# A stand-alone normalisation, from features on partitions to tokens on partitions, in a four-layer kernel

## What is computed

```python
def _layernorm(x, axis=-1, eps=1e-05):
    m = jnp.mean(x, axis=axis, keepdims=True)
    v = jnp.var(x, axis=axis, keepdims=True)
    return (x - m) / jnp.sqrt(v + eps)
...
    h = _layernorm(x, axis=-1) * (1 + cb) + sb
    x = x + gb * _L3_ffn_ref(h, L3_ffn_w_router, L3_ffn_w1, L3_ffn_w2, L3_ffn_w3)
```

## Time and profile before

| | us |
|---|---|
| median of 3 executions | 3686.21 |
| lowest, highest | 3654.16, 3691.45 |
| profiled execution, its own time | 3667.89 |
| its span in the trace | 3666.1 |

### The profile page before, as it was taken

The page is one execution under the profiler, slowest core; times in us unless marked ns, Lnnn a source line. Parts: engine busy times, 40 slices in busy tenths (PEclk is TensorE's granted clock), DMA queues, the critical chain, the costliest instruction groups (busy, mean ns, idle before and its releaser), DMA issues. The chain is left out here.

```text
span 3666.1 us, 70823 instructions
## 1 busy us (share of the span) xinstructions
PE 2720.9 (74%) x20756; PEld 1809.7 (49%) x20756; DVE 2283.8 (62%) x5534; ACT 1324.2 (36%) x3004; POOL 1106.0 (30%) x1121
## 2 busy tenths in 40 slices
PE   5888534228788887878488886888799944478899
PEld 3665433216566565367355554666344711155344
DVE  5776761148888785422367766775555689955455
ACT  1566201005555553323156642564322211123221
POOL 2332107733434332546422223332000244411000
PEclk9999765558999998889679996999899955589999
DMA  3332303334333320346311103331000000000000
GB/s 71 52 49 35 118 36 61 43 78 61 48 47 48 46 38 30 141 104 114 78 24 25 24 11 40 46 51 38 2 1 0 1 3 0 0 7 24 4 0 23
DMA packets 154677, 148.84 MB, mean 41 GB/s; under 512 B 29433, under 2 KB 135555, under 8 KB 149379
## 3 DMA queue, kind: packets, MB, share of 16 engines
q1 hardware_dynamic: 118882, 121.52, 17.1%
q0 software_dynamic: 34336, 21.83, 4.2%
q10 hardware_dynamic: 1152, 1.61, 0.1%
HBM read 52.70 MB, written 33.01 MB: 23 GB/s over the span
## 5 line engine op out<-in xcount | busy, mean ns | idle before, releaser
L569 ACT ACTIVATE a1PR<-bank 128x384 f32<-128x384 f32 x512 | 242.4, 492 | 149.0 <-PE bank L626 145.8
L792 DVE TENSOR_REDUCE a1NM<-bank 128x3 f32<-128x384 f32 x512 | 263.0, 548 | 28.7 <-PE bank L608 27.0
L795 DVE TENSOR_REDUCE a2NMQ<-bank 128x2 f32<-128x512 f32 x256 | 168.3, 685 | 65.5 <-PE bank L612 65.3
L959 PE MATMUL bank<-ONES 128*128 128x256 bf16 x960 | 167.9, 281 | 23.4 <-DMA f3nWR<-in_wr 3.9
L569 ACT ACTIVATE a2PR<-bank 128x512 f32<-128x512 f32 x256 | 149.7, 596 | 96.4 <-PE bank L630 94.3
L1515 POOL TENSOR_TENSOR lM<-lF,lV 128x1024 f32<-128x1024 f32 x32 | 122.2, 3818 | 166.8 <-DVE lF L1528 166.3
L792 DVE TENSOR_REDUCE a4NM<-bank 128x3 f32<-128x384 f32 x256 | 136.1, 552 | 54.8 <-PE bank L608 53.3
L792 DVE TENSOR_REDUCE a0NM<-bank 128x3 f32<-128x384 f32 x256 | 136.8, 553 | 49.4 <-PE bank L608 46.4
L624 PE MATMUL bank<-a1QH,a1KH 128*128 128x128 bf16 x512 | 116.0, 228 | 57.0 <-ACT a1PR L569 42.2
L569 ACT ACTIVATE a4PR<-bank 128x384 f32<-128x384 f32 x256 | 121.2, 489 | 93.9 <-PE bank L626 93.0
L2163 POOL DMA_INDIRECT routed<-yY,yID x80 | 123.6, 1545 | 86.5 <-DMA routed<-yY,yID 40.0
(11 more groups left out here) (676 smaller groups left out, 8708.7 us busy)
## 6 DMA issues: line engine op xcount, KB each, us to landing
yWT<-in_w SPq DMA_DIRECT2D x40, 256.0 KB, 3.0
a1QH<-a1SPL SPq DMA_DIRECT2D x96, 64.0 KB
a1KH<-a1SPL SPq DMA_DIRECT2D x96, 64.0 KB
a1QH<-a1QH SPq DMA_DIRECT2D x96, 64.0 KB
a1KH<-a1KH SPq DMA_DIRECT2D x96, 64.0 KB
rows_by_slot<-gZB SPq DMA_DIRECT2D x5, 1040.0 KB
yXG<-rows_by_slot SPq DMA_DIRECT2D x40, 130.0 KB, 3.1
sums<-rZT SPq DMA_DIRECT2D x2, 2112.0 KB
```

Of the source, the lines that this page charges most:

```text
L569: nc.scalar.activation(PR[:, h % 8, :], bank[2 + h % 2][:, 0:NC], ACT.Exp, scale=SCALE)\
L792: v.tensor_reduce(NM3[:, h, :], S_BANK[h % 3][:, 0:NC].rearrange("p (n k) -> p n k", n=3), AX, ALU.max, negate=True).then_inc(s_used.sem, 1)
L795: v.tensor_reduce(NMQ[:, :, h], S_BANK[h % 3][:, 0:NC].rearrange("p (n k) -> p n k", n=2), AX, ALU.max, negate=True).then_inc(s_used.sem, 1)
L959: pe.matmul(bank[7][:, 0:2 * P], spare[:, 0:P], spare[:, :], start=True, stop=True)
```

## The change

`norm_phase` works with tokens on partitions. A group is 512 tokens (four squares of 128x128), NG = 8 groups. For group g TensorE turns the four squares in (transposition from SRC to PSUM: two squares to EVEN_BANK, three banks deep, two to ODD_BANK, two deep). VectorE takes batch-norm statistics of each square (`bn_stats`: six numbers a token, then `bn_aggr`: mean and variance) and adds eps (VE); without mean it uses variance plus squared mean, in two instructions. POOL raises four columns to -0.5 (RS). VectorE makes NR = -mean x RS, then normalises squares 0 and 1 straight from PSUM as (x - mean) x RS; ScalarE does squares 2 and 3 as x x RS + NR. TensorE turns the four results back (OUT_BANK, two deep), and ScalarE writes the result from PSUM with scale and shift, in two instructions of 256 tokens. Logits, where there are any, are computed from the result, four squares at a time (eight passes), and copied by VectorE. The matmuls of `busy` are gone, everything is unrolled, and only ScalarE (before its first scaling) and TensorE (before its first logits) wait for the phase's loads. Nothing outside `norm_phase` is changed.

```diff
@@ -914,28 +914,26 @@
     nc, bank, SRC, centered = c.nc, c.bank, cfg["nsrc"], cfg["ncentered"]
     E = cfg.get("E", 0) if LG is not None else 0
+    F, NG = 2 * T, NB // 2
+    EVEN_BANK, ODD_BANK, OUT_BANK, LG_BANK = bank[0:3], bank[3:5], bank[5:7], bank[7]
+    place = lambda g, n: (EVEN_BANK[g % 3] if n < 2 else ODD_BANK[g % 2])[:, n % 2 * P:(n % 2 + 1) * P]
     with ExitStack() as ctx:
         sb = lambda name, shape, dt=F32: c.sb(cfg["name"] + "n" + name, shape, dt, ctx)
-        XC, SQ, XN = sb("XC", [P, 4, T]), sb("SQ", [P, 2, T]), sb("XN", [P, T])
-        H = sb("H", [P, 4, T])
...
+        ST, MV = sb("ST", [P, 4, 6]), sb("MV", [P, 2, 4, 2])
+        MM, VE, RS, NR, XN = sb("MM", [P, 4]), sb("VE", [P, 2, 4]), sb("RS", [P, 2, 4]), sb("NR", [P, 2, 4]), sb("XN", [P, 2, 4, P])
         COL, WR = sb("COL", [P, 2]), sb("WR", [P, max(E, 1)])
-        S = signals(c, n_mean=int(centered), n_xc=int(centered), n_sq=1, n_var=1, n_ve=1, n_rs=1, n_dg=1, n_bc=1, n_xn=1,
-                    n_h=1, n_copied=1, n_logits=int(E > 0), n_lg=int(E > 0))
...
+        S = signals(c, n_in=2, n_st=4, n_mv=4, n_ve=1 if centered else 2, n_rs=1, n_nr=1, n_xv=1, n_xa=1, n_out=1, n_h=2,
+                    n_logits=int(E > 0), n_lg=int(E > 0))
+        turned_in, st, mv, ve, rs, nr, xv, xa, turned_out, hr, logits, lg = S
         w_in = c.sem(cfg["name"] + "n_w_in")
         loads = ([(COL[:, 0:1], cfg["ngain"])] if cfg.get("ngain") else []) \
             + ([(COL[:, 1:2], cfg["nshift"])] if cfg.get("nshift") else []) + ([(WR[:, :], cfg["wr"])] if E else [])
-        has = lambda stage, t: not isinstance(t, int) or 0 <= t + stage < NB
-
...
+
+        def gains(b):
+            if cfg.get("ngain"):
+                return COL[:, 0:1], (COL[:, 1:2] if cfg.get("nshift") else 0.0)
+            l, k = cfg["layer"], cfg["nmod"]
+            return c.MOD[:, l, k + 1, one(b)], c.MOD[:, l, k, one(b)]
         block = ctx.enter_context(nc.Block())
@@ -948,116 +946,104 @@
         @block.tensor
         def _(pe):
-            if loads:
-                pe.wait_ge(w_in, 16 * len(loads))
...
+            for t in range(NG + 4):
+                g = t
+                if g < NG:
+                    after(pe, xv, g - 3)
+                    for n in range(4):
+                        if n == 2:
+                            after(pe, xa, g - 2)
+                        mm = pe.transpose(place(g, n), SRC[:, g * F + n * P:g * F + (n + 1) * P], c.ID)
+                        if n % 2:
+                            mm.then_inc(turned_in.sem, 1)
+                g = t - 2
+                if 0 <= g < NG:
+                    after(pe, xv, g)
+                    after(pe, hr, g - 2)
+                    for n in range(4):
+                        if n == 2:
+                            after(pe, xa, g)
+                        mm = pe.transpose(OUT_BANK[g % 2][:, n * P:(n + 1) * P], XN[:, g % 2, n, :], c.ID)
+                    mm.then_inc(turned_out.sem, 1)
+                g = t - 4
+                if E and 0 <= g:
+                    if g == 0:
+                        pe.wait_ge(w_in, 16 * len(loads))
+                    after(pe, hr, g)
+                    after(pe, lg, g - 1)
+                    for n in range(4):
+                        mm = pe.matmul(LG_BANK[:, n * E:(n + 1) * E], NT[:, g * F + n * P:g * F + (n + 1) * P], WR[:, :],
                                        start=True, stop=True)
                     mm.then_inc(logits.sem, 1)
-            steps(pe, step)
         @block.gpsimd
         def _(pool):
-            def step(t, m):
-                if has(-1, t):
...
+            for g in range(NG):
+                after(pool, ve, g)
+                after(pool, xv, g - 2)
+                after(pool, nr, g - 2)
+                nc.gpsimd.tensor_tensor(RS[:, g % 2, :], VE[:, g % 2, :], c.HALF[:, 0:4], ALU.pow).then_inc(rs.sem, 1)
         @block.scalar
         def _(act):
-            def step(t, m):
-                if has(0, t):
...
+            for t in range(1, NG + 3):
+                g = t - 1
+                if g < NG:
+                    after(act, nr, g)
+                    after(act, turned_out, g - 2)
+                    for n in (2, 3):
+                        made = nc.scalar.activation(XN[:, g % 2, n, :], place(g, n), ACT.Identity,
+                                                    bias=NR[:, g % 2, n:n + 1] if centered else 0.0, scale=RS[:, g % 2, n:n + 1])
+                    made.then_inc(xa.sem, 1)
+                g = t - 3
+                if 0 <= g:
+                    if g == 0 and loads:
+                        act.wait_ge(w_in, 16 * len(loads))
+                    after(act, turned_out, g)
+                    for n in range(2):
+                        scale, shift = gains(2 * g + n)
+                        nc.scalar.activation(NT[:, tok(2 * g + n)], OUT_BANK[g % 2][:, n * T:(n + 1) * T], ACT.Identity, bias=shift, scale=scale)\
+                            .then_inc(hr.sem, 1)
         @block.vector
         def _(v):
-            if loads:
-                v.wait_ge(w_in, 16 * len(loads))
...
+            for t in range(NG + 4):
+                g = t
+                if g < NG:
+                    after(v, mv, g - 1)
+                    for n in range(4):
+                        if n % 2 == 0:
+                            after(v, turned_in, g, n // 2 + 1)
+                        v.bn_stats(ST[:, n, :], place(g, n)).then_inc(st.sem, 1)
+                    after(v, xv, g - 2)
+                    for n in range(4):
+                        after(v, st, g, n + 1)
+                        v.bn_aggr(MV[:, g % 2, n, :], ST[:, n, :]).then_inc(mv.sem, 1)
+                g = t - 1
+                if 0 <= g < NG:
+                    after(v, rs, g)
+                    after(v, xa, g - 2)
+                    v.scalar_tensor_tensor(NR[:, g % 2, :], MV[:, g % 2, :, 0], -1.0, RS[:, g % 2, :], ALU.mult, ALU.mult).then_inc(nr.sem, 1)
+                    after(v, turned_out, g - 2)
+                    for n in (0, 1):
+                        made = v.tensor_scalar(XN[:, g % 2, n, :], place(g, n),
+                                               MV[:, g % 2, n, 0:1] if centered else 0.0, RS[:, g % 2, n:n + 1], ALU.subtract, ALU.mult)
+                    made.then_inc(xv.sem, 1)
+                g = t
+                if g < NG:
+                    after(v, mv, g)
+                    after(v, rs, g - 2)
+                    if centered:
+                        v.tensor_scalar(VE[:, g % 2, :], MV[:, g % 2, :, 1], cfg["neps"], None, ALU.add).then_inc(ve.sem, 1)
                     else:
-                        l, k = cfg["layer"], cfg["nmod"]
-                        scale, shift = c.MOD[:, l, k + 1, one(b)], c.MOD[:, l, k, one(b)]
...
+                        v.tensor_tensor(MM[:, :], MV[:, g % 2, :, 0], MV[:, g % 2, :, 0], ALU.mult).then_inc(ve.sem, 1)
+                        after(v, ve, g, 1)
+                        v.scalar_tensor_tensor(VE[:, g % 2, :], MM[:, :], cfg["neps"], MV[:, g % 2, :, 1], ALU.add, ALU.add).then_inc(ve.sem, 1)
+                g = t - 4
+                if E and 0 <= g:
+                    after(v, logits, g)
+                    v.tensor_copy(LG[:, 4 * g:4 * g + 4, 0:E], LG_BANK[:, 0:4 * E].rearrange("p (n e) -> p n e", n=4)).then_inc(lg.sem, 1)
+    close(c, S, NG)
 NT_TILES = NTOK // P
```

## The result

The changed kernel took 3573.68 us (median of 4 executions, 3568.51 to 3579.35), the kernel before 3675.40 beside it (4 executions). The ratio is 0.9726, 95% interval 0.969 to 0.9762: 2.7% faster. The forecast was 3606 us, within 3560 to 3640. The profiled execution took 3568.51 us, its span is 3566.7 us: 99.4 us less than the span before.

The account below looks back on a forecast made before the run. A full TensorE queue, filler included, was taken to bound the norm phases. Gains of 50.9 (without router) + 30.7 (with) - 2 (what follows) = 80 us off 3667.89 gave 3588, or 3606 against the median; range 3560 to 3640.

Parts of the forecast that it names:

- Where the time is: Eight norm phases, each alone between barriers: 315.6 us, 8.6% of the execution, all the change can touch directly.
- What bounded the kernel before: Norm phases before the change: a full TensorE queue, filler included (fillers 167.9 us busy), with other engines waiting for it.
- Unit prices: Instruction costs in the new phase: bn_stats 0.285 us, bn_aggr 0.15, pow of four 1.03, XN 0.41 VectorE, 0.456 ScalarE.
- Rivals 2 and 3: VectorE statistics: dearer, gain 53, 3633 us, chance 0.14; or bn_stats iterating per element, 3741 us, chance 0.05.
- (b): Loop over ODD_BANK, two deep: NR, ScalarE's XN pair, odd pair turned in, statistics, next NR; 2.47 us a group.
- (a): Loop over POOL: VE, pow, NR and both XN before the next VE; 2.1 us a group.
- (c): Loop over OUT_BANK: NR, XN pair, scaling pair, turns out, next pair in, statistics; 5.05 us for two groups, 2.5 each.
- The router phases: f0, f1, f2, f3: TensorE longest at the low clock, 33.2 us each, 132.8 against 163.5, gain 30.7 us.
- The clock: New norm phases: low granted clock, near 0.5, chosen from a row of fp32 transposes; gapless router steps left open.
- Rival 1: Norm phases: the clock stays or becomes high; gain 122 us, 3546 us, or 3564 against the median; chance 0.24.
- The loads' wait: Start of the six phases with loads: TensorE and VectorE no longer wait, about 1.8 us per phase, within the sum.
- Rival 4: Waits between neighbours on one engine and many semaphore waits eat the loops' slack; gain under 37 us, 3650 us; chance 0.07.

Follow-up runs that it names:

- The deeper bank: The changed kernel with ODD_BANK three deep instead of two in the four phases without a router; 3562.69 us, ratio to the kernel before 0.9726.
- shorter ends: Kernel with ODD_BANK three deep, plus VectorE scaling group 5 (no router) and own bank for logits of groups 5 and 7 (router); 3559.92 us, ratio 0.9711.

## Why the prediction was right

**Where the time is** held in the main: 81.6 us were forecast in the eight phases, 89.7 came there. The prediction's sign against it, other phases changing by more than some microseconds, did show in the first pair of profiles (9.7 us) and not in the second profile of the changed kernel (3351.5 against 3348.2). The time itself came out 32 us under the forecast of 3606: 11 of them because the kernel before ran at 3675.4 beside it and not at 3686.2, 8 from the phases, 2 from the cold clock behind the phases that I had charged and no row showed. The other 11 lie outside the phases and have no cause shown; they are within what those stretches vary.

**What bounded the kernel before** was named wrongly. "A full TensorE queue, filler included" would have made h2 shorter without its fillers; it stayed at 37.0, and at the same clock a step took the same 1.91 us. TensorE was busy because it was given something to do in its idle time. The sum did not rest on this, since the new phase was built from nothing.

**Unit prices** held. bn_stats was put at 0.285, from a copy of the same size and the slope to a longer reduction, and measured 0.282; bn_aggr 0.15, measured 0.150; the power 1.03 against 1.007; XN on VectorE 0.41 against 0.404, on ScalarE 0.456 against 0.454. Rivals 2 and 3, dearer statistics and statistics that iterate, fall with this.

**The loops** held as sums: (b) 2.47 against 2.45; (a) 2.1 against 2.00; (c) 5.05 for two groups against 4.75. Their order did not quite: the prediction had (c) longest, at 2.5 a group, and took its period from it; (c) was too dear by 0.15 a group and (b) is the longest. The sums lay 0.05 apart, so the number was hardly touched. The deeper bank showed (a) and then (c). The last period is 1.97 and not 2.5: no further pair is turned in, so (b) is open, and the last NR of h3 waits 1.12 us for POOL, loop (a). That is 0.5 of the 0.9 us by which a phase without a router was shorter than 25.3.

**The router phases** came out at 33.5, 32.5 and 33.2 where 33.2 was forecast, but by luck: two mis-sized terms hid each other. A pass at the low clock was put at 0.24 to 0.245 us start to start; in f3 eight transpositions take 1.74 us and eight router passes 1.57, 0.217 and 0.196 each. So a step is 3.30 and not 3.87; four steps were 12.5 us (3.89, 3.31, 3.30 and 1.97) in place of 15.5. I had divided the 0.98 us of four weight loads by four, which counts the full length of the last one as a step; those four start 0.21 us apart, and the last takes 0.33. And the 2.09 us of eight transpositions hold a wait, which the weight loads of the kernel before show:

```profile
1475.83 0.71 PEld L2037 LDWEIGHTS bank<-CST,HT 128*128 128x128 f32 x4 [0.55 <-ACT gXTM L2025]
1476.82 0.71 PEld L2037 LDWEIGHTS bank<-CST,HT 128*128 128x128 f32 x4 [0.27 <-ACT gXTM L2025]
```

The second four waited for ScalarE. In the changed kernel the first eight of the same line (now L2023) run through in 1.94. Against that stood the end: 10.05 us and not 6.9. I had counted one group's logits behind the last turns out; three stand there, each 1.84 plus 0.38 for the copy of the one before. So the four steps were priced 3.0 us too dear and the end 3.1 us too short.

**The clock.** The forecast took 0.50 from a row of transpositions with short gaps, and the windows show 0.50 to 0.57 in seven phases. f0 had 0.67, with 1.00 from 376 to 385 us, and was 2 us shorter than its forecast. The row that I set against it, 0.97 at 417 to 420, was one in which TensorE was busy 0.44 of 3.00 us, so hardly a transposition ran at it. Rival 1, a high clock throughout, did not occur by itself; the kernel with eight fillers shows what it would have given: 219.4 us, 9 less and not the 42 of rival 1, since fillers also take TensorE's time. Its price for a router phase, 25.6, was not reached either: the least seen was 27.2, f2 at 0.94 with four fillers. The sentence of the Trainium skill ("TensorE: Matmul & The Clock Gate", Part 1) that activity releases the throttle does not foretell these phases if it is read as busy time: in f1 of the changed kernel TensorE was busy 28.25 of 33.00 us and stayed at 0.50, and in h2, less busy, it had 1.00 for three microseconds. With bf16 matmuls of 256 columns between, at 26.25 of 30.40 us busy by the same view, the clock rose to 0.93.

**The loads' wait** went, as forecast. Timeline at the start of f0:

```profile
358.74 0.35 SPq L943 DMA_DIRECT2D f0nWR<-in_wr  x1
...
358.78 1.73 PE L956 MATMUL bank<-CST,XT 128*128 128x128 f32 x7 [1.37 <-PEq L290]
```

TensorE starts as SP issues the load; before, it began 1.8 us behind the phase's start.

**Rival 4**, that waits between neighbours eat the slack, fell: VectorE was never idle before a bn_aggr in the changed kernel.

## What to carry to other kernels

Where engines hand small tiles around, write each ring of waits out as a sum (who must finish before this bank is free again) and compare the rings: the longest sets the period, and the second longest tells what one more buffer is worth: here 0.1 us of 2.45 a period once ring (c) is full, and 0.45 in the three periods before that. Count the periods at both ends separately, since at the end rings open and a queue becomes a chain. Fillers pay where the queue behind them is long and full; at the start and the end of a phase each of them is on the path.

## What the runs showed of the hardware

The less busy of two stretches had the higher clock: 0.50 at 86% busy with fp32 transpositions and passes of 8 columns (f1), 1.00 at 76% busy once eight bf16 matmuls of 256 columns a step were among the transpositions (h3 with fillers). I had left it open for the gapless router steps; they stayed at 0.50 for the whole of f1 and f2, and in f0, whose passes have 64 columns, had 1.00 for 9 us. The same code did not always get the same clock: f1 with shorter ends had 0.50 in one profile and 0.55 in another, and was 0.9 us shorter in the second (32.5 and 31.5). At 0.50 an fp32 transposition of 128x128 costs 0.217 us, start to start, and an fp32 pass over 8 columns 0.196: nearly the same, so a router with few experts, two passes for each square, costs TensorE almost as much as both turns of the data, in and out (1.57 and 1.74 us a group).
